# A graph-attention layer on one core: both load queues given rows and units throughout, and the preparation of the first chunks put in another order

## What is computed

```python
h = jnp.maximum(_layernorm(x, axis=-1), 0.0)
Wh = h @ W
s1, s2 = Wh @ a[:128, 0], Wh @ a[128:, 0]
e = jax.nn.leaky_relu(s1[:, None] + s2[None, :], negative_slope=0.2)
masked = jnp.where(adj > 0, e, NEG_INF)
attention = jax.nn.softmax(masked, axis=1)
out = x + jax.nn.elu(attention @ Wh)
```

## Time and profile before

| | |
|---|---|
| time, median of 3 runs | 986.88 us (984.89 to 987.04) |
| the profiled execution's own time | 986.53 us |
| its span, first to last instruction | 984.8 us |
| PE busy, share of the span | 957.8 us, 97% |
| DVE, ACT, POOL busy | 847.4, 530.2, 61.1 us |
| mean granted TensorE clock, share of full speed | 0.986 |
| HBM read and written | 275.84 MB and 4.23 MB, 284 GB/s over the span |

### The profile page before, as it was taken

The page is one execution under the profiler, slowest core; times in us unless marked ns, Lnnn a source line. Parts: engine busy times, 40 slices in busy tenths (PEclk is TensorE's granted clock), DMA queues, the critical chain, the costliest instruction groups (busy, mean ns, idle before and its releaser), DMA issues.

```text
span 984.8 us, 21358 instructions
## 1 busy us (share of the span) xinstructions
PE 957.8 (97%) x8447; PEld 952.4 (97%) x8447; DVE 847.4 (86%) x848; ACT 530.2 (54%) x366; POOL 61.1 (6%) x140
## 2 busy tenths in 40 slices
PE   5879999999999999999999999999999999999997
PEld 4879999999999999999999999999999999999997
DVE  5879889898888988899888988889888998889885
ACT  3478754575646544565445655465445654546521
POOL 3456400000000000000000000000000000000000
PEclk7799999999999999999999999999999999999999
DMA  9999999999999999999979999999999999999900
GB/s 242 266 307 309 311 287 258 311 284 327 355 332 294 270 354 297 291 268 304 345 199 343 320 341 315 296 280 273 354 300 290 268 320 331 299 298 268 273 0 24
DMA packets 276950, 280.77 MB, mean 285 GB/s; under 512 B 9696, under 2 KB 272032, under 8 KB 276896
## 3 DMA queue, kind: packets, MB, share of 16 engines
q1 hardware_dynamic: 141072, 144.92, 53.8%
q10 hardware_dynamic: 135824, 135.18, 49.4%
HBM read 275.84 MB, written 4.23 MB: 284 GB/s over the span
## 4 chain that ended last, share of the span: by engine, by line
PE 93%; DMA 3%; DVE 2%; ACT 1%; issue 1%; POOL 1%; ACTq 0%; SPq 0%; DVEq 0%; POOLq 0%
PE ps L1150 90%; DMA raw<-in_adj 2%; PE ps L1107 1%; PE ps L1180 1%; PE ps L1097 1%; DMA xs<-in_x 0%; ACT gate L473 0%; PE ps L1158 0%; DVE stats L662 0%; DVE big L699 0%; ACT obuf L425 0%; ACT big L433 0%; POOL scale L346 0%; POOL root L343 0%; POOL root L344 0%
## 5 line engine op out<-in xcount | busy, mean ns | idle before, releaser
L1150 PE MATMUL ps<-wh,weights 128*128 (+1 forms) x8016 | 901.0, 275 | 3.6 <-DVE weights L799 3.6
L1150 PEld LDWEIGHTS ps<-wh,weights 128*128 128x128 f32 x8016 | 899.2, 192 | 4.2 <-issue 3.8
L799 DVE SCALAR_TENSOR_TENSOR weights<-big,beta 128x1024 f32<-128x1024 f32 x504 | 636.4, 1275 | 106.7 <-PE ps L1150 105.2
L473 ACT ACTIVATE gate<-raw 128x4096 uint8<-128x4096 int32 x126 | 456.6, 3623 | 364.2 <-DVE big L770 287.9
L770 DVE STREAM_TRANSPOSE big<-gate 128x1024 int32<-128x1024 int32 x126 | 156.1, 1239 | 5.2 <-ACT gate L473 5.0
L505 ACT ACTIVATE big<-ps,rden 128x128 f32<-128x128 f32 x56 | 23.0, 412 | 13.0 <-issue 13.0
L506 ACT ACTIVATE big<-ps,rden 128x128 f32<-128x128 f32 x56 | 23.4, 418 | 0.0
L1189 PE MATMUL ps<-wh,weights 128*128 128x129 f32 x128 | 18.5, 308 | 1.9 <-DVE weights L787 1.9
L1189 PEld LDWEIGHTS ps<-wh,weights 128*128 128x128 f32 x128 | 17.8, 223 | 2.3 <-issue 2.1
L1107 PE MATMUL ps<-wext,big 128*128 128x130 f32 x128 | 17.8, 295 | 2.0 <-ACT big L433 2.0
L1107 PEld LDWEIGHTS ps<-wext,big 128*128 128x128 f32 x128 | 16.8, 209 | 2.4 <-issue 2.4
(11 more groups left out here) (111 smaller groups left out, 171.2 us busy)
## 6 DMA issues: line engine op xcount, KB each, us to landing
raw<-in_adj ACTq DMA_DIRECT2D x256, 512.0 KB, 11.5
raw<-in_adj SPq DMA_DIRECT2D x256, 512.0 KB, 11.9
out_x<-obuf SPq DMA_DIRECT2D x28, 128.0 KB, 10.6
xs<-in_x SPq DMA_DIRECT2D x26, 128.0 KB, 10.6
big<-r_rows SPq DMA_DIRECT2D x6, 512.0 KB, 14.7
xs<-in_x ACTq DMA_DIRECT2D x6, 128.0 KB, 4.2
out_x<-obuf SPq DMA_DIRECT2D x6, 64.0 KB, 1.7
out_x<-obuf ACTq DMA_DIRECT2D x2, 64.0 KB, 2.2
```

Of the source, the lines that this page charges most:

```text
L473: nc.scalar.activation(gate[:, u % GATE_SLOTS, :, :], raw[:, u % RAW_SLOTS, :, :], ACT.Sign)\
L799: nc.vector.scalar_tensor_tensor(weights[:, v % WT_SLOTS, :], rbc[:, half, :], beta[:, bass.ds(jt, 1)], turned_bytes[:, chunk, v // QUAD, ...
L1150: ins = nc.tensor.matmul(to, weights[:, u % WT_SLOTS, t * P:(t + 1) * P], moving, start=start and opens, stop=stop, skip_group_check=True)
```

## The change

The rows of chunks 3 to 7 are loaded half by SP and half by ScalarE (before: all by SP), behind units 2, 3, 5, 7 and 9. ScalarE issues its half of unit 2 in its head. Chunk 0 is normalised by ScalarE (2 of the 4 tiles of each group) and GpSimd (the other 2); VectorE no longer takes part. ScalarE forms the bound on the scores ahead of `relu(0)`, and an Exp of one column stands ahead of `source_factors(0)`, so that the exponentials' table is loaded there. VectorE takes `first_words` and its transpose ahead of `take_products(0)` and `z_of_products(1)`. `products(0)` stands ahead of the branch. TensorE's warm-up products are 6 + 9 + 3 + 4 instead of 10 + 4. The steps of chunks 2 to 7 that prepare them stand at other places.

```diff
+    ROWS_BEHIND = {2: 3, 3: 4, 5: 5, 7: 6, 9: 7}
...
             for u in range(2, RAW_SLOTS):
                 load_unit(sp, 0, u, (0, 1))
-                load_rows(EARLY + u - 1)
+                load_rows(ROWS_BEHIND[u], (0, 1))
...
-                    if u % 2 == 0 and EARLY + 1 + u // 2 < CHUNKS:
-                        load_rows(EARLY + 1 + u // 2)
+                    if u in ROWS_BEHIND:
+                        load_rows(ROWS_BEHIND[u], (0, 1))
...
             pool.wait_ge(norm_ready, 1)
-            normalise(0, 1)
+            normalise(0, 0, GROUP // 2)
+            normalise(0, 1, GROUP // 2)
...
             deviations(0)
+            load_unit(act, 0, 1, (2,))
 
             normalise(0, 0, GROUP // 2)
-            load_unit(act, 0, 1, (2,))
-            relu(0)
+            normalise(0, 1, GROUP // 2)
             act.wait_ge(norms_done, 1)
             nc.scalar.activation(bound[:, :], ps[:, 1, 0:2], ACT.Sqrt, scale=float(F)).then_inc(bound_ready, 1)
+            relu(0)
             load_unit(act, 0, 1, (3,))
             deviations(1)
             relu(1)
+            load_unit(act, 0, 2, (2, 3))
...
                     load_unit(act, ahead // UNITS, ahead % UNITS, (2, 3))
+                    load_rows(ahead)
+
+                def load_rows(u):
+                    if u in ROWS_BEHIND:
+                        for group in (2, 3):
+                            load_x(act, ROWS_BEHIND[u], group)
+
+                def take_table():
+
+                    act.wait_ge(bound_ready, 1)
+                    nc.scalar.activation(spare[:, :], bound[:, 0:1], ACT.Exp, scale=-1.0)
 
                 def first_band():
+                    take_table()
                     source_factors(0)
                     exp_half(0)
                     source_factors(1)
+                    relu(2)
                     second_words()
-                    relu(2)
-                    load_ahead(0)
+                    load_rows(2)
                     exp_half(1)
                     relu(3)
                     load_ahead(1)
...
                         if u == 1:
                             source_factors(2)
                             source_factors(3)
+                        if u == 2:
                             relu(4)
-                        if u == 2:
                             relu(5)
                         if u == 3:
                             source_factors(4)
                             source_factors(5)
-                        if u == 4:
                             normalise(3, 0)
                             normalise(3, 1)
+                        if u == 4:
+                            relu(6)
                         if u == 5:
                             exp_rows(1)
-                            relu(6)
+                            relu(7)
                         if u == 6:
-                            relu(7)
                             normalise(4, 0)
                             normalise(4, 1)
...
             variances(0)
-            deviations(0)
-            dve.wait_ge(norm_ready, 1)
-            for t in range(GROUP // 2, GROUP):
-                ins = nc.vector.tensor_scalar(xn[0][:, t, :], xs[:, t, :], scale[:, t:t + 1], shift[:, t:t + 1],
-                                              ALU.mult, ALU.add)
-            ins.then_inc(xn_dve, 1)
...
+            deviations(0)
             for part in range(2):
                 statistics(1, part)
...
-                        if v == 5:
-                            statistics(3, 0)
+                        if v in (4, 5):
+                            statistics(3, v - 4)
                         if v == 6:
                             turn_ahead(2)
-                    statistics(3, 1)
+                        if v == 7:
+                            seeds(3)
                     turn_ahead(3)
...
-                            if c == 1 and v == 0:
-                                seeds(3)
...
+                            if c + 3 < CHUNKS and v in (0, 2):
+                                statistics(c + 3, v // 2)
+                            if c + 3 < CHUNKS and v == 5:
+                                seeds(c + 3)
...
                 z_of_products(0)
+                first_words()
+                link(turn_words(0, 0, 0, 0))
                 take_products(0)
                 z_of_products(1)
-                first_words()
-                link(turn_words(0, 0, 0, 0))
                 first_band()
...
             turn(0)
-            pe.wait_ge(squares_ready, 1)
-            nc.tensor.matmul(ps[:, 1, 0:2], ones[:, :], squares[:, :], start=True, stop=True).then_inc(norms_done, 1)
             turn(1)
+            products(0)
...
-                        if v == 1:
+                        if v == 3:
                             turn(4)
-                        if v == 3:
+                        if v == 6:
                             turn(5)
                         multiply_half(v, 1, weights_ready, weights_used)
...
-                            if u == (4 if c == 1 else 3 if c == 2 else 1) and n < CHUNKS:
+                            if u == (4 if c == 1 else 3) and n < CHUNKS:
                                 turn(2 * n)
-                            if u == (5 if c > 2 else 6) and n < CHUNKS:
+                            if u == 6 and n < CHUNKS:
                                 turn(2 * n + 1)
```

More of the change, by code:

```diff
@@ L123, in graph_attention @@
         nmax = sb("nmax", [P, 1])
+        spare = sb("spare", [P, 1])
         ps = ctx.enter_context(nc.psum_tensor("ps", [P, 8, 512], F32))
@@ L150, in graph_attention @@
         late_ready, seed_ready = sem("late_ready"), sem("seed_ready")
-        norm_ready, xn_act, xn_dve, xn_pool = sem("norm_ready"), sem("xn_act"), sem("xn_dve"), sem("xn_pool")
+        norm_ready, xn_act, xn_pool = sem("norm_ready"), sem("xn_act"), sem("xn_pool")
         xt_ready, ht_ready = sem("xt_ready"), sem("ht_ready")
@@ L226, in _, with load_rows @@
         def _(sp):
-            def load_rows(k):
-                for group in range(4):
+            def load_rows(k, groups):
+                for group in groups:
                     load_x(sp, k, group)
@@ L279, in general_path @@
                 for k in range(EARLY + 1 + RAW_SLOTS // 2, CHUNKS):
-                    load_rows(k)
+                    load_rows(k, range(4))
                 for k in range(RAW_SLOTS):
@@ L313, in _, with normalise @@
             nc.gpsimd.memset(mean_rows[:, :, :], 0.0).then_inc(consts, 1)
[L315 to L318, removed]
+            def normalise(n, odd, skip=0):
+                row = [P, GROUP - skip, F]
+                t = slice((2 * n + odd) * GROUP + skip, (2 * n + odd + 1) * GROUP)
+                to = xn[n % 2][:, odd * GROUP + skip:(odd + 1) * GROUP, :]
                 link(nc.gpsimd.tensor_tensor(to, xs[:, t, :], mean[:, t].unsqueeze(2).to_broadcast(row), ALU.subtract))
@@ L616, in general_path @@
             def general_path():
-                for u in range(2, RAW_SLOTS):
-                    load_unit(act, 0, u, (2, 3))
+                load_unit(act, 0, 3, (2, 3))
+                for k in (3, 4):
+                    for group in (2, 3):
+                        load_x(act, k, group)
                 for n in range(1, CHUNKS):
@@ L893, in first_band @@
                                 turn_ahead(2 * c + 1 + v // 3)
-                            if c == 1 and v == 0:
-                                seeds(3)
                             if c == 1 and v in (1, 2):
                                 take_products(v + 3)
-                            if c == 1 and v in (2, 4):
-                                statistics(4, v // 2 - 1)
-                            if c == 1 and v == 5:
-                                seeds(4)
-                            if c == 1 and v in (6, 7):
-                                statistics(5, v - 6)
+                            if c + 3 < CHUNKS and v in (0, 2):
+                                statistics(c + 3, v // 2)
+                            if c + 3 < CHUNKS and v == 5:
+                                seeds(c + 3)
                             if c >= 2 and c + 1 < CHUNKS and v in (5, 6):
                                 take_products(2 * c + v - 3)
-                            if c >= 2 and c + 3 < CHUNKS and v == 1:
-                                seeds(c + 3)
-                            if c >= 2 and c + 4 < CHUNKS and v in (2, 4):
-                                statistics(c + 4, v // 2 - 1)
                             if (c, v) == (CHUNKS - 2, 2):
@@ L1067, in _ @@
         def _(pe):
-            pe.wait_ge(consts, 4)
-            pe.wait_ge(w_in, 16)
-            nc.tensor.transpose(ps[:, 4, 0:P], wext[:, 0:F], identf[:, :]).then_inc(wt_turned, 1)
             def warm(count):
@@ L1076, in warm @@
                                      mean_rows[:, :, :].rearrange("p t f -> p (t f)"), start=True, stop=True)
-            warm(10)
+            pe.wait_ge(consts, 4)
```

(19 more changed lines are left out.)

## The result

The changed kernel takes 983.15 us (median of 20 runs, 981.07 to 986.66) beside 985.94 for the kernel before (20 runs, 984.68 to 988.10): a ratio of 0.9971 [0.9962, 0.9981], 2.8 us less. Forecast were 983.0 us and a gain of 3.6. The profiled execution took 984.68 us, 1.5 more than the median.

A forecast was written before the change was run, and what follows sets the result against it. TensorE bounds the kernel, busy 906.68 of 912.76 us from 72.04 on. Step 7 of chunk 1 at 70.2 instead of 73.83 gains 3.6: 986.53 - 3.6 = 982.9, with the median 0.35 higher, stated as 983.0; range 980.0 to 986.2.

The forecast's parts named there:

- Only the last wait in band 0 counts: Band 0: the change can only move the moment from which TensorE never waits again, 72.04 us before; bands 1 to 7 untouched.
- The head at nothing: Kernel start: the head's edits gain 0, as first gates wait for unit 0, landing at 20.4; first half step stays at 23.5.
- `turn(4)` still behind GpSimd: Band 0, first half's end: GpSimd's normalised rows of chunk 2 still hold `turn(4)` until 41.3, cost 0.
- Gate of unit 3 at 47.4: ScalarE, second half: gate right behind `relu(5)`, no transfer wait, at 47.4 instead of 49.77, with low clock for half the stretch.
- Chunk 1 at 53.6: TensorE starts chunk 1 at 53.6 us instead of 56.13, after unit 3's gate, turn and weigh.
- Gate of unit 5 behind `relu(6)`, at 64.1: ScalarE in chunk 1: gate follows `relu(6)` at 64.1 instead of 66.36, giving step 7 at 70.2 instead of 73.83.
- Step 0 at low clock costs 1.2 more: Start of chunk 1 on TensorE: the low clock adds 1.2 us to step 0, before `turn(6)` ends at 63.3.
- No wait of TensorE after 70: Sign of being right: TensorE waits no more after 70 us, with step 7 of chunk 1 at 70.2.
- The queues fed throughout: Loads, near 22 to 31 us: no gap in ScalarE's queue; both queues fed move 341 GB/s, one alone 196.
- One pipe: Rival: 196 GB/s has another cause or ScalarE's queue empties later; unit 5 3.1 us late, gain 2.5, 984.0. Chance 0.10.
- Held by `relu(5)`: Rival: TensorE at 1.2 GHz puts `relu(5)` at 48.5, gate of unit 3 at 49.7; gain 0.8, 985.7. Chance 0.13.
- Unit 0 late: Rival: SP's small bandwidth share delays unit 0 to 21.5 or 28.5, holding everything behind; at worst 991.0. Chance 0.06.

The follow-up runs named there:

- products first: Kernel after with VectorE's old head order, `take_products(0)` and `z_of_products(1)` ahead of `first_words`: 981.05 us, ratio 0.9958 to the kernel before.
- the zero products: Kernel after with 18 products of zeros filling TensorE's wait ahead of chunk 1: 981.32 us, ratio 0.9954 to the kernel before.
- the moved steps alone: Kernel after with all loads as they were before the change, only steps and head changed: 985.46 us, ratio 0.9993 to the kernel before.
- the fastest: Kernel after with products first, the zero products, `relu(6)` behind unit 5's gate, ScalarE's unit 5 load earlier, chunk 2's statistics and seeds earlier: 978.60 us, ratio 0.9924.
- the loads alone: Kernel before with only the change's new loads, no computation step moved: 986.61 us, ratio 1.0006 to the kernel before.
- the second profile: Kernel after run again without an edit in a later batch: 982.62 us, ratio 0.9962 to the kernel before.
- unit 2 late again: Kernel after with ScalarE's half of unit 2 issued behind the second words again, not in its head: 987.81 us, ratio 1.0013 to the kernel before.

## Why the prediction was right, point by point

**Only the last wait in band 0 counts: right, and it holds in every profile but one.** From step 7 of chunk 1 to the end pass 911.0 us before (73.83 to 984.8), 910.8 after (72.22 to 983.0), 911.1 with products first (65.97 to 977.1), 911.1 with the zero products (68.41 to 979.5), 911.0 with the moved steps alone (73.34 to 984.3) and 911.8 in the fastest (64.06 to 975.9, with a later wait of 0.45). The exception, the loads alone, has 913.5 and the later waits that go with it. (VectorE's sum for a chunk, 16.9 in the forecast, adds up to 17.0, TensorE's own time: there was nothing to spare, yet no wait came of it after.)

**The head at nothing: right in mechanism, mis-sized by 1.3 us.** Unit 0 covers the early table load and `products(0)`, as the run with both late shows. But unit 0 landed at 19.40, not at 20.4, and the first half step was weighed at 22.22, not 23.5. Nor is VectorE's new order worth nothing: the old one weighs it at 21.54.

**`turn(4)` still behind GpSimd: right,** at 40.25, as the head's 1.3 us went through statistics and GpSimd (its first row group starts at 37.69, before at 38.76). Forecast was 41.3.

**Gate of unit 3 at 47.4: right by two misses that cancel.** It began at 47.53. TensorE started a microsecond earlier, but ran at half clock for nearly all of the stretch (39.5 to 46.3), where I had taken half of it.

**Chunk 1 at 53.6: right** (53.88, and 53.10 in the second profile).

**Gate of unit 5 behind `relu(6)`, at 64.1: right in mechanism, mis-sized.** The term that failed is "Step 0 at low clock costs 1.2 more", for which the forecast gives no row (7.14 us less 5.79 would be 1.4): it measured 2.7 in the first profile and 1.5 in the second. The gate came at 66.11 and at 64.06, step 7 at 72.22 and at 70.16, against a forecast of 70.2. This term is not a constant of the kernel but differs between executions: the two spans, 983.0 and 981.0, lie 1.8 and 3.8 below that of before, on both sides of the 2.8 of the medians, and the forecast of 3.6 lies within that spread. The Trainium skill (TensorE: Matmul & The Clock Gate, Part 1: The HAM clock gate) says of the slow matmuls at the start of a kernel that one kernel shows different numbers of them from run to run. Behind a wait in mid-kernel the 8.51 and 7.24 us of the same 48 records agree.

**No wait of TensorE after 70: wrong by the same term.** The wait at 72.22 is that of step 7, 2 us late, not a new one.

**The queues fed throughout: wrong,** as shown above (28.5 to 30.9 and 48.4 to 53.9 us). It cost nothing here. The reading behind it was incomplete: ScalarE's queue was called empty from 22.5 to 30 us because unit 2 is issued only at 24.18. That explains the first 1.7 us; for the rest, DMAs had been issued and did not move until 31.15. Issuing unit 2 in the head was the right step either way.

**The time of 983.0: in part luck.** The head's 1.3 us, not counted, stands against a low clock that cost more than forecast, and of the two spans the first shows half of the 3.6. The sum itself is 982.9 + 0.35 = 983.3, not 983.0; the 983.15 measured lies between.

**The rivals.** *One pipe*: the gates of units 3 and 5 waited for no transfer, and 346 GB/s with both queues against 199 and 202 with one was seen again (ScalarE's queue, all but alone at 73 to 76 us after, moved 201). The rule of the Trainium skill (DMA: Bandwidth & Descriptors, "Issuing engines are not separate DMA queues"), that more issuers save issue time alone, is not what these traces show. Why one queue stops near 200 stays open; the packets were of about 1 KB throughout, and no run here varies that. *Held by `relu(5)`*: it began at 46.95, not 48.5, though at half clock as that rival had it. *Unit 0 late*: it landed at 19.40.

What no step of the prediction had asked is what each half is worth alone. I had put the gain down to a sum of steps; the two runs with one half each show that it needs both.

## What to carry to other kernels

Find the moment from which the bounding engine never waits again, and price a change by how far it moves that moment. A chain of waits gives way only where all its links do: freeing one transfer moved the start of chunk 1 by 2.3 us and the end by nothing. Issue a queue's next load well before the queue runs out: here up to 7.0 us passed from an issue to the first packet that it moved. Where TensorE's wait is followed by a low clock, look at it over several executions, and try to fill or shorten the wait: the low clock cost up to 2.7 us here, as much as the change brought. And hold a profile's time against the median of its kernel before reading a size from it.

## What the runs showed of the hardware that I had not expected

One load queue moved 196 to 202 GB/s and two 341 to 346, with all 16 DMA engines shown as busy in both cases. Where ScalarE's queue had stopped moving for over 1 us, its next packet started 4.4 to 7.0 us after the issue of the DMA that it belongs to (31.15 for 24.18 before, 53.94 for 47.04 and 70.06 for 65.62 after); the first DMA of the kernel took 1.2 us (issued at 0.86, first packet at 2.02 before). Around such stretches an issue took up to 4.9 us instead of 0.6 (4.77 before, 4.88 with the loads alone), and with unit 2 late again issues held ScalarE's computation for 8.66 us. And the stretches at 1.2 GHz after the same wait of 3.40 us lasted differently long in two executions of one kernel: 48 records took 8.51 and 7.24 us, and 5.79 in the profile of products first, with the same wait of 3.40 in front.
